# A two-layer decoder on one core: head groups packed into one PSUM bank with one evacuation per item, and bulk loads issued by GpSimd from tables laid out by partition

## What is computed

```python
x = _layernorm(x + _L0_attn_ref(x, Wq, Wk, Wv, Wo))            # rotary embedding, softmax attention
x = _layernorm(x + _L0_xattn_ref(x, ctx_1024, ctx_1024))       # causal, a slope per head, no projections
x = _layernorm(x + _L0_ffn_ref(x, ...))                        # 64 tokens per 512 picked by a router, attention and gated FFN on them
x = _layernorm(x + _L1_attn_ref(x, ...))                       # attention with a Gaussian bias
x = _layernorm(x + _L1_xattn_ref(ctx_1024, ctx_1024, x, mask, ...))  # masked cross attention
x = _layernorm(x + _L1_ffn_ref(x, ...))                        # 8 experts, the best 2 of each token
```

```python
scores = jnp.einsum('bhqd,bhkd->bhqk', q, k) / jnp.sqrt(jnp.float32(D))
probs = jax.nn.softmax(scores, axis=-1)
ctx = jnp.einsum('bhqk,bhkd->bhqd', probs, v)
```

## Time and profile before

| | us |
|---|---|
| median of 3 runs | 976.7 (976.18 to 982.54) |
| the profiled execution's own time | 972.38 |
| its span, first to last instruction | 970.5 |
| PE busy | 763.2 (79%) |
| DVE busy | 604.1 (62%) |
| ACT busy | 498.5 (51%) |
| POOL busy | 232.1 (24%) |

### The profile page before, as it was taken

One profiled execution on the slowest core, in us unless ns is written; L12 is line 12 of the kernel. 1 busy time (PEld: TensorE's weight loads), 2 busy tenths in 40 slices (PEclk: granted clock), 3 DMA queues, 4 the chain that ended last, 5 costly groups with the idle time before them and its releaser, 6 DMA issues.

```text
span 970.5 us, 20640 instructions
## 1 busy us (share of the span) xinstructions
PE 763.2 (79%) x7108; PEld 416.7 (43%) x7109; DVE 604.1 (62%) x1908; ACT 498.5 (51%) x847; POOL 232.1 (24%) x390
## 2 busy tenths in 40 slices
PE   2687888999996645866749999999999529999950
PEld 1232323454443332434412333333334429999950
DVE  1476878667665823336348988877885344555576
ACT  1146767656556321512706877666656326665620
POOL 3344522223010120100501132323100062404223
PEclk8588999999998865956957999999999759999985
DMA  5466452242201123000532222221200611212212
GB/s 118 105 194 204 121 157 77 73 125 58 69 24 62 33 65 76 13 1 1 154 91 72 72 58 77 83 62 51 68 20 2 260 50 47 78 50 70 64 49 62
DMA packets 76075, 75.57 MB, mean 78 GB/s; under 512 B 21377, under 2 KB 65153, under 8 KB 75217
## 3 DMA queue, kind: packets, MB, share of 16 engines
q1 hardware_dynamic: 73504, 67.18, 24.1%
q0 software_dynamic: 2480, 7.21, 2.3%
HBM read 50.66 MB, written 23.13 MB: 76 GB/s over the span
## 4 chain that ended last, share of the span: by engine, by line
PE 61%; DVE 16%; ACT 5%; POOL 5%; issue 5%; DMA 4%; SPq 3%; POOLq 0%; DVEq 0%; ACTq 0%
PE PS L616 12%; PE PS L682 12%; PE PS L1874 8%; PE PS L633 8%; DVE MS L787 5%; PE PS L696 4%; PE PS L1884 4%; PE PS L328 2%; PE PS L623 2%; ACT X L1113 2%; POOL experts_x L1785 2%; PE PS L1047 1%; SPq L882 1%; DVE CX L804 1%; DMA OT<-experts_x 1%
## 5 line engine op out<-in xcount | busy, mean ns | idle before, releaser
L787 DVE TENSOR_REDUCE MS<-PS 128x2 f32<-128x512 f32 (+2 forms) x448 | 250.3, 592 | 130.3 <-PE PS L633 63.1
L745 ACT ACTIVATE BIG<-PS 128x1024 f32<-128x1024 f32 (+2 forms) x288 | 259.8, 906 | 63.2 <-PE PS L623 38.2
L616 PE MATMUL PS<-BIG 62*128 62x256 bf16 (+1 forms) x1088 | 199.3, 277 | 73.5 <-DMA BIG<-rows_k 16.5
L623 PE MATMUL PS<-BIG 64*128 64x256 bf16 (+1 forms) x1088 | 183.9, 269 | 1.2 <-DMA BIG<-MT 1.2
L682 PE MATMUL PS<-BIG,VA 128*32 128x256 f32 (+1 forms) x2176 | 166.7, 379 | 3.4 <-ACT OT L738 3.2
L616 PEld LDWEIGHTS PS<-BIG 62*128 62x128 bf16 x1088 | 68.5, 95 | 206.1 <-issue 97.2
L738 ACT COPY OT<-PS 128x256 f32<-128x256 f32 (+1 forms) x144 | 51.8, 360 | 117.3 <-PE PS L682 117.2
L1874 PE MATMUL PS<-OT,VA 128*128 128x128 f32 x736 | 96.7, 279 | 0.4 <-ACT OT L1931 0.4
L1874 PEld LDWEIGHTS PS<-OT,VA 128*128 128x128 f32 x736 | 91.4, 196 | 0.6 <-ACT OT L1931 0.6
L851 POOL CAST MB<-MS 128x16 bf16<-128x16 f32 (+1 forms) x72 | 14.2, 198 | 294.7 <-DVE MS L787 158.2
L682 PEld LDWEIGHTS PS<-BIG,VA 128*32 128x32 f32 x2176 | 43.4, 109 | 74.5 <-issue 63.7
(11 more groups left out here) (238 smaller groups left out, 1062.6 us busy)
## 6 DMA issues: line engine op xcount, KB each, us to landing
rows_q<-parts SPq DMA_DIRECT2D x32, 192.0 KB, 2.1
rows_k<-parts SPq DMA_DIRECT2D x32, 192.0 KB, 2.1
BIG<-rows_q SPq DMA_DIRECT2D x64, 96.0 KB
BIG<-rows_k SPq DMA_DIRECT2D x64, 96.0 KB
BIG<-in_ex_w SPq DMA_DIRECT2D x3, 2048.0 KB, 12.1
BIG<-rows_q SPq DMA_DIRECT2D x64, 64.0 KB
BIG<-rows_k SPq DMA_DIRECT2D x64, 64.0 KB
OT<-experts_x SPq DMA_DIRECT2D x46, 64.0 KB, 1.8
```

Of the source, the lines that this page charges most:

```text
L616: return nc.tensor.matmul(bank[:, first:first + kw], g.Q6[b.buf][rows, u, qt * P:(qt + 1) * P], g.K6[b.buf][rows, u, 0:kw], start=start, s ...
L623: return nc.tensor.matmul(g.bank[2 * (v % 2) + a][:, core.offset[kt]:core.offset[kt] + n], g.K6[b.buf][rows, v, kt * P:(kt + 1) * P], g.Q6 ...
L745: nc.scalar.activation(g.PT[v // 2 % 2][:, 2 * (v % 2):2 * (v % 2) + 2, 0:w], g.bank2[v % 2][:, :, 0:w], ACT.Exp, scale=SCALE).then_inc(se ...
L787: nc.vector.tensor_reduce(g.MS[:, 0:n, a, u], self.ring_bank["mx", step, a][:, 0:n * w] .rearrange("p (n k) -> p n k", n=n), axis=AX_X, op ...
```

## The change

Three parts.

1. *Values and context of an item.* The four head groups of an item now go to one bank and stay there. A head still has 32 weight columns, but it uses only one half of them (W2 = 16): heads 0 to 7 (q = 0) the first half, heads 8 to 15 (q = 1) the second, zeros in the other; group 2q + o writes columns S·o on. So groups 0 and 2 add into the first 256 columns, groups 1 and 3 into the other 256. There is one evacuation per item, of 512 columns, one wait of PE for it per item (before the next item's first group), 4 transposes, and one context step with one reciprocal over 32 columns and two multiplications, at the end of step 1. POOL writes the value rows of an item in two instructions, one for each q, instead of one (a1, with a bias row: four instead of two). The column order of the values (VFIRST) is set on the host.
2. *Loads.* The mask, CTXT, weights, X, CTX and the tables are issued by POOL at the same steps; the 19 tables are packed in two arrays (9.4 KB and 3 KB a partition) and come at steps 28 and 32 in place of 40, 42 and 44. X, CTX, the mask and the output are laid out by partition in DRAM.
3. *The start.* The two first_rest of the first q and k go from POOL to DVE (after both rotations), and k of item 0 is loaded by ACT's queue, behind ACT's last cast.

The core of the diff:

```diff
+W2 = PVW // 2
-    def first_rest(self, pool, n):
+    def first_rest(self, eng, nc_eng, n):
...
             def values(n, kt):
-                after(pe, self.ot_done, n)
+                if grp == 0:
+                    after(pe, self.ot_done, b.k)
+            q, o = divmod(grp, 2)
             for hh in range(4):
                 last = nc.tensor.matmul(
-                    g.bank[6][PVW * hh:PVW * hh + PVW, lo:lo + w],
-                    g.VA[b.par][:, kt, 8 * (hh % 2) + 2 * grp + hh // 2, :],
+                    g.bank[6][PVW * hh:PVW * hh + PVW, S * o + lo:S * o + lo + w],
+                    g.VA[b.par][:, kt, 8 * q + 4 * (hh % 2) + 2 * o + hh // 2, :],
                     g.PT[grp % 2][:, hh, core.offset[kt]:core.offset[kt] + w],
-                    start=kt == 0, stop=kt == core.nqt - 1)
+                    start=grp == 0 and kt == 0, stop=grp == 3 and kt == core.nqt - 1, skip_group_check=True)
...
-            for grp in (2 * half, 2 * half + 1):
-                last = nc.tensor.transpose(g.bank[7][:, grp * P:(grp + 1) * P], g.OT[b.par][:, grp, qt * P:(qt + 1) * P],
-                                           g.ident[:, :])
+            for o in range(2):
+                last = nc.tensor.transpose(g.bank[7][:, (2 * qt + o) * P:(2 * qt + o + 1) * P],
+                                           g.OT[b.par][:, o, qt * P:(qt + 1) * P], g.ident[:, :])
...
-            nc.scalar.copy(g.OT[b.par][:, grp, 0:w], g.bank[6][:, 0:w]).then_inc(self.ot_done.sem, 1)
+            nc.scalar.copy(g.OT[b.par][:, 0:2, 0:w], g.bank[6].rearrange("p (o t) -> p o t", o=2)[:, :, 0:w])\
+              .then_inc(self.ot_done.sem, 1)
...
-            v = step - self.LAG
-            if v % 2 == 0:
-                evacuate(v // 2 - 2)
+            if v % 8 == 2 and self.item(items, v // 8 - 1):
+                evacuate(self.items[v // 8 - 1])
...
-            line.first_loads(sp, core_a0.items)
+            line.load(sp, core_a0.items[0], "q")
+            line.load(sp, core_a0.items[1])
...
             split_a0.second_part(act, 1)
+            line.load(act, core_a0.items[0], "k")
...
             split_a0.rotate(dve, 1)
+            split_a0.first_rest(dve, nc.vector, 0)
+            split_a0.first_rest(dve, nc.vector, 1)
...
-                if step == 21:
-                    sp.dma_start(g.X[:, :, :], io["x"].rearrange("(t p) d -> p t d", p=P)).then_inc(x_in.sem, 16)
+                if step == 21:
+                    pool.dma_start(g.X[:, :, :], io["x"]).then_inc(x_in.sem, 16)
...
+                if step in (28, 32):
+                    n = step // 4 - 7
+                    pool.dma_start(g.tables[F32 if n == 0 else BF16][:, :], io[f"tables_{n}"]).then_inc(tables_in.sem, 16)
```

More of the change, by code:

```diff
@@ L598, in turns_of @@
         k, n = divmod(step - self.LAG - 14, 8)
-        b = self.item(items, k)
-        qt, half = {0: (0, 0), 1: (0, 1), 3: (1, 0), 4: (1, 1)}.get(n, (2, 0))
-        return (b, qt, half) if b and qt < b.core.nqt else (None, 0, 0)
+        return (self.item(items, k), n) if n < 2 else (None, 0)
     def maxima_of(self, items, step):
@@ L720, in tensor @@
                 turn_m(b, half)
-            b, qt, half = self.turns_of(items, step)
+            b, qt = self.turns_of(items, step)
             if b:
-                turn_context(b, qt, half)
+                turn_context(b, qt)
             if side:
@@ L812, in vector @@
                     join(bm, step % 8 // 4)
-            b, qt, half = self.turns_of(items, step)
-            if b and half == 1:
-                context(b, qt)
+            b, turn = self.turns_of(items, step)
+            if b and turn == 1:
+                context(b)
             if side:
@@ L2538, in _ @@
             for buf in g.VA:
[L2539 removed]
+                for q in range(2):
+                    last = nc.gpsimd.memset(buf[:, :, 8 * q:8 * q + 8, W2 * q + DH:W2 * q + DH + 1], 1.0)
             last.then_inc(va_zeroed.sem, 1)
```

204 lines of the change are left out of this document (101 added, 103 removed).

## The result

The changed kernel takes 969.7 us (median of 14 runs, 966.2 to 975.0), the kernel before beside it 978.4 (14 runs, 974.6 to 984.4). The ratio is 0.991 with a 95% interval of 0.989 to 0.993: 9 us faster, where 31 were forecast, and outside the range. The profiled execution took 966.8 us, its span is 965.0, 5.5 less than before's.

A forecast was written before the change was run, and what follows sets the result against it. The prediction took PE's matmuls to bound most of x0 and x1, with DVE sharing a1. Savings of 21.4, 8.5 and 3.4 less 0.3 made 33.0 us; keeping 2 back gave 976.7 − 31.0 = 945.7, range 934 to 961.

The forecast's parts named there:

- A PE instruction removed there shortens the kernel by its own time until DVE comes next: In 160:300 and 610:750, mostly x0 and x1, nearly all of the chain is matmuls, so removed PE time counts in full.
- The transposes: Over a0, x0, a1 and x1, removing half the transposes of OT saves half their chain time, 15.4 us.
- the reciprocals: One DVE reciprocal per item instead of two, counted in 16 items of a0 and a1: 3.0 us saved, bounds 0 to 5.
- the give-back: The longer context step on DVE costs 0.25 us in each of 16 items of x0 and x1: 4.0 us, bounds 0 to 6.4.
- The ends: At the ends of x0 and x1, one copy and one context step shorten the tail: 2.5 us saved at each.
- PE's wait for the copy to OT: PE's first group of the next item waits for ACT's longer copy: costed at 0, bounds 0 to 6 us.
- Part 2, 8.5: In a0, loads leaving SP save 6.0 us of waits for MT and 2.5 of slow clock: bounds 2 to 11.
- Part 3, 3.4: At the start, k is written 2.2 us earlier and lands 3.0 us after issue: 3.4 us saved, bounds 1.2 to 5.6.
- The rival that k waits for q's transfers after all: At the start, k's load waits in the DMA engines, leaving only 2.2 us from the earlier write; no separate chance given.
- DVE binds: In x0 and x1, DVE's maxima bind once a pair of transposes goes, losing half of 12.2 us: 954, chance 0.14.
- the loads still collide: In a0, MT still waits beside X, the mask and tables, so moving the loads brings 2 us: 952, chance 0.14.
- The burst decides: At step 1 of an item, PE loses DVE's context step and ACT's copy, 1.6 us an item: 991, slower; chance 0.05.

The follow-up runs named there:

- short: The changed kernel with DVE's maxima of x0 over half the columns, PE's work unchanged: 957.2 us, ratio 0.976 to the kernel before.
- split_apart: The changed kernel with the context in two pieces, the second pair of transposes and its piece four steps after the first: 963.2 us, ratio 0.983 to before.
- part1: The kernel before with only the edits to values, copy, transposes, context and value rows: 970.3 us, ratio 0.989 to before.
- part2: The kernel before with only bulk loads on POOL's queue, layouts by partition and packed tables: 969.8 us, ratio 0.990 to before.
- part3: The kernel before with only the start's edits (k of item 0 on ACT's queue, rests of q and k on DVE): 977.6 us, ratio 0.998 to before.
- after_mt_all: The changed kernel with X, the mask's second half, the tables and CTX issued only behind landed MT rows: 960.1 us, ratio 0.981 to before.
- best_bias: The changed kernel with context pieces four steps apart, bulk loads behind MT, item 1's loads behind item 0's, first-half bias earlier in x0 and f0: 959.9 us, ratio 0.978.

## Why the prediction was wrong

- **"A PE instruction removed there shortens the kernel by its own time until DVE comes next"** is the step that failed. In x0's short steps DVE came next at once: the pair at step 4 was worth 0.03 us, the one at step 3 0.22, where the chain gives a pair 0.37. The transposes (15.4), the reciprocals (3.0) and the give-back (4.0) were to bring 14.4 us in a0, x0, a1 and x1. Part 1 alone moves these stages by +0.4, +0.3, +0.5 and −2.0. For x0 the loop over two banks is shown as the cause, by short and split_apart. For a0 and a1 the runs show that the gain is missing, and that split_apart finds 1.3 us in a1, but not which wait took it. The chain named PE because each PE row starts where the one before ends. A PE matmul's end in the profile is a model (the page says so), so a short wait for a bank hides in a matmul's length. The Trainium skill, Perfetto Trace Analysis, Tensor Engine Instruction, says the same of the end time. In the step after shown above, the pair of transposes is gone and PE's rows leave only 0.13 us uncovered. In seven items of x0 the trace lists 0.7 us of waits for DVE's maxima after (0.9 before); short took 0.2 to 0.4 us out of three of an item's four steps with short values.
- **The give-back of 4.0** was about right: splitting the piece again returned 3.4 in x0 and x1. The reciprocal was mis-sized, 354 ns and not 280.
- **The ends**: x1 3.9 for 2.5, x0 3.4 for 2.5, right in kind and somewhat small. f0's 2.0 are not seen: the distances of its four items are 8.8, 9.6 and 10.3 us in part1 as in part2 and part3 (only before has 9.4 and 8.0 in place of the last two, at its higher clock).
- **PE's wait for the copy to OT**, costed at 0 with a bound of 6: in the whole trace 5.1 us in place of 3.2. Right.
- **Part 2, 8.5**: 0.3 of the 7.5 us of waits went. I said that MT would be issued sooner (right) and leave 1.5 us (wrong), because I priced SP's order and not what the new order puts in flight. The Trainium skill's rule on queues taken in turn (DMA: Bandwidth & Descriptors, Queues, rings and completion order) did not protect MT as I read it: in SP's queue, behind the loads of q, it took 9.6 us to land beside 2 MB in POOL's. The clock's share (2.5) did not come either: in 90:100, after the wait, the granted clock is 0.67.
- **Part 3, 3.4**: 0.8 lost. The landing of 3.0 "as now" is the term that was wrong: alone behind q it took 3.07, beside q and item 1 5.78 (6.06 in part3). The 2.2 us of the earlier write were right. part3 has them; in the changed kernel's profile the write is only 1.1 sooner, because ACT's cast of k's first part starts only at 15.66 there, and not at 14.29. The rival that k waits for q's transfers after all is the one that came in kind, but even its 2.2 us did not reach the first score matmul (0.4 in part3).
- **The rivals.** "DVE binds" (954) and "the loads still collide" (952) were both true, and the start with them. I gave the first two together 0.05 at 960 to 967, and the measured 969.7 lies above even that. They were not independent chances: each came from the same reading, that an engine or queue which looks free is free. "The burst decides" did not come: its price was 0.22 an item in x0, not 1.6.

By its own tests: transposes halved (right), copies of 580 ns (right), first score matmul at 26 (30.4), no wait for MT over 2 us (6.7), the clock at 1.00 through 90 to 150 (0.67 in 90:100, 1.00 in 100:150), a1 and x1 with its end to shrink by 8 (5.4), PE's wait for the copy to OT under 6 us (5.1).

## What to carry to other kernels

Before pricing an instruction off the busiest engine, measure the period of a step in steps with and without it: where both are equal, something else holds the loop, and its removal is worth nothing. A ring of two banks has its own period (the consumer's two pieces plus the way back), and extra work on the consumer is free only up to its idle time in a step, so short pieces in different steps beat one long one. Giving bulk loads a queue of their own takes them out of an order that also protected small urgent transfers; here it paid to tie them to the landing of those instead. When the gains of the parts do not add up to that of the whole, compare the stages that repeat exactly before explaining the sum.

## What was not expected of the hardware

- A transfer of 4 KB on SP's queue took 9.6 us to land while two of 1 MB were in flight on POOL's; with at most one beside it the waits for it vanished (after_mt_all).
- A change from matmuls of 128 rows to halves of 62 rows costs some 0.1 us (best_bias).
- The stage between f0's last item and a1 has nearly the same work in all kernels and took 100.3 to 102.5 us in seven profiles, 105.8 to 107.4 in six, and 110.4 in best_bias. The granted clock separates the sizes: in the last 40 us of the stage it is 0.78 to 0.80 in the seven shorter ones and 0.63 to 0.65 in the other seven. The windows 475:500 and 500:525 of before and of after show it:

```profile
475.00:500.00 25.00, 10.16 (x61) 6.85 (x60) 5.86 (x17) 7.38 (x15) 7.25 (x7) 0.68 0.57 157
500.00:525.00 25.00, 21.62 (x134) 5.56 (x134) 21.35 (x34) 7.92 (x12) 4.21 (x12) 0.56 0.16 46
```

```profile
475.00:500.00 25.00, 12.19 (x53) 9.78 (x51) 4.15 (x13) 5.09 (x10) 3.31 (x4) 0.50 0.46 121
500.00:525.00 25.00, 20.71 (x118) 5.15 (x118) 20.05 (x31) 5.96 (x8) 4.14 (x14) 0.53 0.21 56
```

  After runs at 1.2 GHz (0.50) in all of the first window, before for a part of it at 2.4. What decides it was not tried. Both the slower clock and the time are of the same executions, and whether a kernel always gets the same size is open too: the profiles are one execution each. The difference is over half of the whole gain, so one profile's span against another's says little below 5 us; the stages at full clock say more.
